# Attention output computed transposed: values stationary, probabilities moving, two heads on the array's column halves

## The chip, the cores and the metric

The kernel runs on one core of a Trainium2 chip. The metric is the device time of one execution in microseconds (us), the median of several runs. The engines are TensorE (PE: matmuls, with their weight loads listed as PEld), VectorE (DVE), ScalarE (ACT), GpSimd (POOL) and the DMA queue of SyncE (SP).

## The reference

For each of 32 batch elements: x is 256 rows of 256, the context 77 rows of 256. Both are layer-normalized; queries come from x, keys and values from x and context together (333 keys). There are 4 heads of 64. Queries and keys are RMS-normalized per head, context keys may be masked, and softmax attention follows:

```python
sim = einsum('bhid,bhjd->bhij', qn, kn)
attn = softmax(where(mask, sim, -max), axis=-1)
out = einsum('bhij,bhjd->bhid', attn, v)
x = x + out.reshape(b, n, 256) @ W_out + b_out
x = x + ffn(layernorm(x))
```

The feed-forward part is a mixture of 8 experts (squared ReLU, 128 inner columns each, the best two of a group by a sigmoid router) and a shared expert of 512 inner columns.

## The kernel before, in words

The kernel makes 32 steps, one for each batch element (B = 32). A step b does the attention of element b, the feed-forward part of element b-1, and the projections (keys, values, queries) of element b+1. The order of instructions on each engine is written out by hand in the five `step` functions; engines meet only through semaphores, whose counts are computed from b. Steps 0, 1 and 31 are written out, steps 2 to 30 are the body of one loop (`steps`, line 212).

Sizes: P = 128; S = 256 query rows make T = 2 tiles; D = 256 makes FT = 2 feature tiles of two heads each; 333 keys make CH = 3 chunks of KC = 111. A unit u is one tile of 128 queries for one head; there are U = 8 of them, u = 4 t + h. A pair is two units of the same tile, with heads 2 ft and 2 ft + 1.

Most matrix products are split (`split_product`, line 258): both operands are held as a high and a low part of type fp32r, and three matmuls (L261, L262, L263) add up. The transposes, and the product of probabilities and values, work on plain fp32.

Attention of a step, in the order of TensorE: transposes of the normalized keys (L321), sums of query squares (L309), four score pairs (L342, L344, L346; the two heads of a pair use the upper and the lower 64 rows of the array), then per unit u the transposes of its probabilities (`transpose_probs`, L356), three chunks of 128 x 111, and `probs_times_v` (L367), which has the transposed probabilities stationary and the 64 value columns of the head moving, so that unit u fills 64 columns of the bank `attn_ps[:, 3]`. After unit 7 DVE multiplies the whole bank by the inverse row sums (`attn_out`, L834), TensorE transposes the result (`transpose_attn`, L380), ACT takes the high parts (L626), DVE the low parts (`attn_low`, L840), and `project_out` (L384) multiplies with W_out into the bank `attn_ps[:, 3]`. DVE adds the residual (L848) and makes the second layer norm.

Between these pieces stand, in TensorE's queue, those of the feed-forward part: `up(p)` for six pairs of hidden tiles (12 matmuls of 256 columns), the shared expert's `down_shared` (12 matmuls each), `down_expert(e)` (6 matmuls each), and, towards the end of the step, the next element's `transpose_ln` (L275, L276), `project_kv` of the key chunks 1, 2 and 0 (6 matmuls of 512 columns each) and `project_q`.

ACT copies the transposed probabilities out of PSUM (`pt_out`, L618, ring `probs_t`, 3 slots), makes the exponentials (`softmax`, L611, with the row sums as a by-product), the ReLU and its square (`hidden`, L644, L649), and the next element's scaled normalized rows (`ln_full`, L570). DVE's queue has, after the scores are masked (`mask_scores`, L815) and among router steps: `layer_norm1`, additions of the experts' results (`add_expert`, L972), the rounding of hidden values (`hidden_high`, L957), `ln_high` (L760), then `invert_sums` (L827, the reciprocal of 8 row sums per partition), `add(4)`, `attn_out`, `add(5)`, `attn_low`, `k_norms` (L780, L785), `layer_norm2`. POOL makes low parts of hidden values and inverse roots.

Of the kernel before, what the change touches and what calls it, by code (L numbers as in the profile page):

```python
# [22 lines left out]
ALU = mybir.AluOpType  # L23
# [10 lines left out]
def build(nc, x, ctx_in, mask, g_x, b_x, g_l, b_l, q_gamma, k_gamma, w_q, w_kv, w_out, b_out,  # L34
          gate_t, gate_bias, up_t, down_t, out):
    B, S, D = x.shape
# [20 lines left out]
    with ExitStack() as stack:  # L57
# [59 lines left out]
        row_inv = sb("row_inv", [P, U])  # L117
        PT_RING = 3
        SCORE_RING = 4
        probs_t = sb("probs_t", [KC, PT_RING, CH * P])  # L120
        attn = sb("attn", [P, U, DH])
# [60 lines left out]
        score_ps, pt_ps, pv_ps = sem("score_ps"), sem("pt_ps"), sem("pv_ps")  # L182
        at_ps, out_ps, x2t_ps, logit_ps = sem("at_ps"), sem("out_ps"), sem("x2t_ps"), sem("logit_ps")
# [5 lines left out]
        prob_done, pt_done = sem("prob_done"), sem("pt_done")  # L189
# [15 lines left out]
        PARTS = (slice(1, 3), slice(0, 1))  # L205
        LN1_STEPS = 2 * (T + 1)
# [15 lines left out]
        def _(sp):  # L222
# [28 lines left out]
            steps(sp, step)  # L251
# [5 lines left out]
        def _(pe):  # L257
# [102 lines left out]
            def probs_times_v(b, u, first):  # L360
                if u == 0:
# [10 lines left out]
            def transpose_attn(b, following):  # L372
                pe.wait_ge(attn_done, b + 1)
# [4 lines left out]
                for ft in range(FT):  # L378
                    for t in range(T):
                        last = nc.tensor.transpose(up_ps[:, ft, t * P:(t + 1) * P],  # L380
                                                   attn[:, t * H + 2 * ft:t * H + 2 * ft + 2, :], ident[:])
                    last.then_inc(at_ps, 1)

            def project_out(b):  # L384
                pe.wait_ge(at_hi_done, (b + 1) * FT)
                pe.wait_ge(at_lo_done, (b + 1) * FT)
                for t in range(T):
                    for k in range(FT):
                        cols = slice(t * P, (t + 1) * P)
                        last = split_product(attn_ps[:, 3, t * D:(t + 1) * D], (at_hi[:, k, cols], at_lo[:, k, cols]),  # L390
                                             (w_hi[:, k, 3 * D:4 * D], w_lo[:, k, 3 * D:4 * D]), k == 0, k == FT - 1)
                last.then_inc(out_ps, 1)
# [72 lines left out]
            def step(b, experts, following):  # L465
# [773 lines left out]
```

## Time and profile before

| | us |
|---|---|
| median of 3 runs | 1362.79 |
| lowest and highest | 1362.51, 1364.13 |
| the profiled execution, its own time | 1370.73 |
| its span, first to last instruction | 1368.9 |
| PE busy, weight loads busy | 1286.9, 1194.2 |
| DVE, ACT, POOL busy | 1022.7, 747.5, 539.4 |
| L367, products of probabilities and values (1536 passes) | 205.7 |
| L356, transposes of probabilities (768) | 132.5 |

How to read it: busy time is what an engine's instructions cover. Matmuls are pipelined, and their ends are modelled, so that the starts of successive ones say more than their durations. A row of the timeline gives the start, the duration from the first start to the last end, engine, line, operation, what is written and read, shapes, and how many instructions were merged; in brackets stands how long the engine was idle before it and what ended that.

### The profile page before, as it was taken

The numbers are of one execution on the slowest core, as the hardware profiler recorded it, in microseconds if no ns is written. First come the engines' busy times: TensorE is split into PE (matmuls) and PEld (weight loads), VectorE is DVE, ScalarE is ACT, GpSimd is POOL, SyncE is SP. The second block draws the span as 40 slices with busy tenths as digits, with TensorE's granted clock in tenths as the row PEclk, the third lists the DMA queues.
The fourth block names the chain that finished last, engine by engine and source line by source line (L and its number), as shares of the span: only waits on it lengthen the run. The fifth ranks groups of instructions, "written<-read, shape, count | busy, mean of one in ns | idle before, by whom it ended". The sixth has DMA issues, their size and how long they took to land.

```text
span 1368.9 us, 33442 instructions
## 1 busy us (share of the span) xinstructions
PE 1286.9 (94%) x10176; PEld 1194.2 (87%) x10176; DVE 1022.7 (75%) x3465; ACT 747.5 (55%) x1701; POOL 539.4 (39%) x477
## 2 busy tenths in 40 slices
PE   3799999999999999999999999999999999999997
PEld 2788899898899898899898899888889889889986
DVE  3478777788777778777778877777877778877765
ACT  3465555565555565555565555555555556555552
POOL 4143443343443343344343343333444334444332
PEclk9599999999999999999999999999999999999998
DMA  4000000000000000000000000000000000000000
GB/s 137 11 12 20 19 18 0 18 18 18 18 18 0 18 18 18 18 18 8 10 18 18 18 18 8 10 18 18 18 18 13 5 18 18 18 18 18 0 9 16
DMA packets 28099, 24.20 MB, mean 18 GB/s; under 512 B 6640, under 2 KB 27536, under 8 KB 28080
## 3 DMA queue, kind: packets, MB, share of 16 engines
q1 hardware_dynamic: 27744, 23.83, 5.5%
q0 software_dynamic: 336, 0.14, 0.2%
q8 instruction: 10, 0.16, 0.0%
q14 instruction: 9, 0.07, 0.0%
HBM read 15.57 MB, written 8.39 MB: 18 GB/s over the span
## 4 chain that ended last, share of the span: by engine, by line
PE 68%; DVE 13%; issue 12%; ACT 4%; DVEq 1%; POOL 1%; DMA 1%; POOLq 0%; ACTq 0%
PE attn_ps L367 13%; PE up_ps L261 6%; PE up_ps L263 6%; PE up_ps L262 6%; PE down_ps L261 5%; PE attn_ps L356 5%; PE attn_ps L261 5%; PE attn_ps L262 4%; PE attn_ps L263 4%; PE down_ps L263 4%; PE down_ps L262 4%; DVE masked L815 4%; PE attn_ps L309 2%; ACT relu L649 2%; ACT relu_sb L644 1%
## 5 line engine op out<-in xcount | busy, mean ns | idle before, releaser
L1148 POOL TENSOR_TENSOR hid_lo<-relu,hid_hi 128x512 fp32r<-128x512 f32 x192 | 246.6, 1284 | 485.1 <-DVE hid_hi L957 485.1
L261 PE MATMUL down_ps<-down_hi,hid_hi 128*128 128x256 f32 x768 | 238.4, 310 | 17.7 <-POOL hid_lo L1148 16.1
L972 DVE SCALAR_TENSOR_TENSOR acc<-down_ps,route_w,acc 128x256 f32<-128x256 f32 x512 | 222.0, 476 | 22.4 <-PE down_ps L263 17.7
L261 PE MATMUL up_ps<-x_hi,up_hi 128*128 128x256 f32 x768 | 230.3, 300 | 1.2 <-ACT x_hi L633 1.0
L263 PE MATMUL down_ps<-down_hi,hid_lo 128*128 128x256 f32 x768 | 215.9, 281 | 0.0
L262 PE MATMUL down_ps<-down_lo,hid_hi 128*128 128x256 f32 x768 | 215.7, 281 | 0.0
L262 PE MATMUL up_ps<-x_lo,up_hi 128*128 128x256 f32 x768 | 215.5, 281 | 0.0
L263 PE MATMUL up_ps<-x_hi,up_lo 128*128 128x256 f32 x768 | 215.5, 281 | 0.0
L367 PE MATMUL attn_ps<-v_sb,probs_t 111*128 111x64 f32 x1536 | 205.7, 275 | 10.0 <-DVE row_max L815 9.3
L611 ACT ACTIVATE probs<-masked,neg_max,q_scale 128x333 f32<-128x333 f32 x256 | 167.8, 656 | 79.0 <-DVE neg_max L822 79.0
L367 PEld LDWEIGHTS attn_ps<-v_sb,probs_t 111*128 111x128 f32 x1536 | 194.7, 196 | 16.8 <-DVE row_max L815 15.6
L957 DVE CAST hid_hi<-relu 128x512 fp32r<-128x512 f32 x192 | 113.9, 593 | 113.8 <-ACT relu L649 113.7
L644 ACT ACTIVATE relu_sb<-up_ps 128x512 f32<-128x512 f32 x192 | 114.7, 597 | 142.9 <-PE up_ps L263 141.0
L261 PEld LDWEIGHTS down_ps<-down_hi,hid_hi 128*128 128x128 f32 x768 | 145.6, 190 | 32.9 <-issue 32.9
L1105 POOL TENSOR_TENSOR k_scale<-k_norm,minus_half 111x8 f32<-111x8 f32 x64 | 84.5, 1322 | 186.0 <-DVE k_norm L785 186.0
L618 ACT ACTIVATE probs_t<-attn_ps 111x384 f32<-111x384 f32 x256 | 124.4, 486 | 59.1 <-PE attn_ps L356 59.1
L261 PEld LDWEIGHTS up_ps<-x_hi,up_hi 128*128 128x128 f32 x768 | 146.4, 191 | 8.0 <-issue 6.6
L356 PE MATMUL attn_ps<-ident,probs 128*111 128x128 f32 x768 | 132.5, 283 | 15.6 <-DVE row_max L815 14.7
L262 PEld LDWEIGHTS up_ps<-x_lo,up_hi 128*128 128x128 f32 x768 | 146.4, 191 | 0.0
L263 PEld LDWEIGHTS up_ps<-x_hi,up_lo 128*128 128x128 f32 x768 | 146.2, 190 | 0.0
L262 PEld LDWEIGHTS down_ps<-down_lo,hid_hi 128*128 128x128 f32 x768 | 145.8, 190 | 0.0
L263 PEld LDWEIGHTS down_ps<-down_hi,hid_lo 128*128 128x128 f32 x768 | 144.6, 188 | 0.0
(145 smaller groups left out, 2819.3 us busy)
## 6 DMA issues: line engine op xcount, KB each, us to landing
x_in<-in_x SPq DMA_DIRECT2D x32, 256.0 KB, 2.7
out<-acc SPq DMA_DIRECT2D x32, 256.0 KB, 2.2
c_in<-in_ctx SPq DMA_DIRECT2D x32, 77.0 KB
up_stage<-in_up_t SPq DMA_DIRECT2D x1, 1536.0 KB, 12.1
down_stage<-in_down_t SPq DMA_DIRECT2D x1, 1536.0 KB, 15.0
mask_in<-in_mask SPq DMA_DIRECT2D x32, 9.6 KB, 2.8
w_stage<-in_w_kv SPq DMA_DIRECT2D x1, 512.0 KB, 5.8
w_stage<-in_w_q SPq DMA_DIRECT2D x1, 256.0 KB, 5.1
```

The lines of the kernel that those rows point to most:

```text
L261: nc.tensor.matmul(out_ap, s_hi, m_hi, start=first, stop=False)
L262: nc.tensor.matmul(out_ap, s_hi, m_lo, start=False, stop=False)
L263: return nc.tensor.matmul(out_ap, s_lo, m_hi, start=False, stop=last)
L356: last = nc.tensor.transpose(attn_ps[0:KC, u % PT_RING, c * P:(c + 1) * P], probs[:, u, c * KC:(c + 1) * KC], ident[:])
L367: last = nc.tensor.matmul(attn_ps[:, 3, u * DH:(u + 1) * DH], probs_t[:, u % PT_RING, c * P:(c + 1) * P], v_sb[:, c, h * DH:(h + 1) * DH], ...
L611: nc.scalar.activation(probs[:, u, :], masked[:, u, :], ACT.Exp, bias=neg_max[:, u:u + 1], scale=q_scale[:, u:u + 1], accum_out=row_sum[:, ...
L618: nc.scalar.activation(probs_t[:, u % PT_RING, :], attn_ps[0:KC, u % PT_RING, 0:CH * P], ACT.Copy).then_inc(pt_done, 1)
L644: nc.scalar.activation(relu_sb[:, p % 2, :], up_ps[:, p % 2, :], ACT.Relu).then_inc(relu_done, 1)
L957: nc.vector.tensor_copy(hid_hi[:, p % HID_RING, :], relu2[:, p % 2, :]).then_inc(hid_hi_done, 1)
L972: nc.vector.scalar_tensor_tensor(acc[:, t, :], down_ps[:, (e + 1) % 2, t * D:(t + 1) * D], route_w[:, t, e:e + 1], acc[:, t, :], ALU.mult, ...
L1105: nc.gpsimd.tensor_tensor(dst, src, minus_half[0:src.shape[0], 0:src.shape[1]], ALU.pow).then_inc(done, 1)
L1148: nc.gpsimd.tensor_tensor(hid_lo[:, p % HID_RING, :], relu2[:, p % 2, :], hid_hi[:, p % HID_RING, :], ALU.subtract).then_inc(hid_lo_done, 1)
```

## The change

1. `probs_times_v` works on pairs. The values of a head (111 x 64) are stationary, the transposed probabilities (111 x 128) move. The two heads of a pair write to the partitions 0 to 63 and 64 to 127 of the same bank and the same columns, so each uses one half of the array's columns. The result is already transposed: features on partitions, queries along the free dimension.
2. The inverse row sums must then vary along the free dimension. `invert_sums` is called once per query tile and writes each inverse 64 times (128 x 4 x 64). `spread_inverse` (4 transposes on TensorE, in `up_ps[:, 0]`) turns them, `inverse_out` (ACT) copies them to `inv_t`, and `attn_out` multiplies by that. `transpose_attn` is gone.
3. `attn_high` and `attn_low` work by query tile, out of SBUF. `project_out` is called once per tile, and writes to `up_ps[:, 1]`; the second call stands after the projection of chunk 2.
4. The ring of transposed probabilities in SBUF has 4 slots instead of 3 (`PT_SB`); that in PSUM keeps 3.
5. The loop is gone: all 32 steps are written out.

```diff
-        row_inv = sb("row_inv", [P, U])
+        row_inv = sb("row_inv", [P, U, DH])
...
-        def steps(eng, step):
-            step(0, False, True)
-            step(1, True, True)
-            with eng.Fori(2, B - 1) as b:
-                step(b, True, True)
-            step(B - 1, True, False)
+        def steps(step):
+            for b in range(B):
+                step(b, b > 0, b < B - 1)
...
-            def probs_times_v(b, u, first):
...
-                pe.wait_ge(pt_done, b * U + u + 1)
-                h = u % H
+            def probs_times_v(b, pair):
+                t, ft = divmod(pair, FT)
...
+                pe.wait_ge(pt_done, b * U + 2 * pair + 2)
+                cols = slice(ft * S + t * P, ft * S + (t + 1) * P)
                 for c in range(CH):
-                    last = nc.tensor.matmul(attn_ps[:, 3, u * DH:(u + 1) * DH],
-                                            probs_t[:, u % PT_RING, c * P:(c + 1) * P],
-                                            v_sb[:, c, h * DH:(h + 1) * DH], start=(c == 0), stop=(c == CH - 1))
+                    for i in range(2):
+                        h = 2 * ft + i
+                        last = nc.tensor.matmul(attn_ps[i * DH:(i + 1) * DH, 3, cols],
+                                                v_sb[:, c, h * DH:(h + 1) * DH],
+                                                probs_t[:, (2 * pair + i) % PT_SB, c * P:(c + 1) * P],
+                                                start=(c == 0), stop=(c == CH - 1))
...
+            def spread_inverse(b, following):
+                pe.wait_ge(row_inv_done, (b + 1) * T)
+                if following:
+                    pe.wait_ge(ln_full_done, (b + 1) * FT + 1)
+                else:
+                    pe.wait_ge(relu_done, b * PAIRS)
+                for t in range(T):
+                    for ft in range(FT):
+                        u = t * H + 2 * ft
+                        last = nc.tensor.transpose(up_ps[:, 0, ft * S + t * P:ft * S + (t + 1) * P],
+                                                   row_inv[:, u:u + 2, :], ident[:])
+                last.then_inc(inv_ps, 1)
...
                 transpose_probs(b, 1)
-                probs_times_v(b, 0, first)
                 ffn("down", 0)
                 transpose_probs(b, 2)
-                probs_times_v(b, 1, first)
+                probs_times_v(b, 0)
                 ffn("up", 4)
                 transpose_probs(b, 3)
-                probs_times_v(b, 2, first)
                 ffn("down", 1)
                 transpose_probs(b, 4)
-                probs_times_v(b, 3, first)
+                probs_times_v(b, 1)
                 ffn("down", 2)
                 transpose_probs(b, 5)
                 ffn("up", 5)
-                probs_times_v(b, 4, first)
                 ffn("down", 3)
+                probs_times_v(b, 2)
                 if following:
                     transpose_ln(b + 1, experts)
-                probs_times_v(b, 5, first)
                 transpose_probs(b, 6)
                 ffn("down", 4)
                 transpose_probs(b, 7)
                 ffn("down", 5)
-                probs_times_v(b, 6, first)
-                probs_times_v(b, 7, first)
+                spread_inverse(b, following)
+                probs_times_v(b, 3)
                 if following:
                     project_kv(b + 1, 1)
-                transpose_attn(b, following)
+                project_out(b, 0, following)
                 if following:
                     project_kv(b + 1, 2)
-                project_out(b)
+                project_out(b, 1, following)
                 if following:
                     project_kv(b + 1, 0)
...
+            def inverse_out(b, first):
+                act.wait_ge(inv_ps, b + 1)
...
+                nc.scalar.activation(inv_t[:], up_ps[:, 0, :].rearrange("p (f s) -> p f s", f=FT),
+                                     ACT.Copy).then_inc(inv_done, 1)
...
-            def invert_sums(b):
-                dve.wait_ge(prob_done, b * U + U)
-                nc.vector.reciprocal(row_inv[:], row_sum[:]).then_inc(row_inv_done, 1)
+            def invert_sums(b, t, first):
+                cols = slice(t * H, (t + 1) * H)
+                dve.wait_ge(prob_done, b * U + (t + 1) * H)
+                if not first:
+                    dve.wait_ge(inv_ps, b)
+                nc.vector.reciprocal(row_inv[:, cols, :], row_sum[:, cols].unsqueeze(2)
+                                     .to_broadcast([P, H, DH])).then_inc(row_inv_done, 1)
...
                 routing(18)
+                invert_sums(b, 0, first)
                 add(0)
...
                     ln_high(b + 1, False)
-                invert_sums(b)
+                invert_sums(b, 1, first)
                 add(4)
                 attn_out(b, first)
                 add(5)
-                attn_low(b)
+                attn_low(b, 0)
+                attn_low(b, 1)
```

## Rows read from the trace of the kernel before

**Rows 1.** Busy time by stretch, one whole step of the loop (x: instructions).
```profile
core 0: us, PE busy (x) PEld busy (x) DVE busy (x) ACT busy (x) POOL busy (x), PEclk, DMA share, GB/s
...
604.30:645.15 40.85, 39.53 (x320) 36.75 (x319) 31.66 (x109) 23.07 (x53) 16.64 (x14) 1.00 0.05 15
```

**Rows 2.** Timeline of PE: key transposes and first probability transposes, loop and last step.
```profile
604.34 0.74 PE L321 MATMUL attn_ps<-ident,k_rms 111*128 111x111 f32 x6
...
618.11 0.58 PE L356 MATMUL attn_ps<-ident,probs 128*111 128x128 f32 x3 [0.54 <-DVE row_max L815]
...
1298.72 0.74 PE L321 MATMUL attn_ps<-ident,k_rms 111*128 111x111 f32 x6
...
1312.29 0.55 PE L356 MATMUL attn_ps<-ident,probs 128*111 128x128 f32 x3 [0.59 <-ACT probs L611]
```

**Rows 3.** Timeline of PE, 624.5 to 639.1 of the same step, in part.
```profile
624.58 0.49 PE L356 MATMUL attn_ps<-ident,probs 128*111 128x128 f32 x3
624.90 0.78 PE L367 MATMUL attn_ps<-v_sb,probs_t 111*128 111x64 f32 x6
625.49 0.36 PE L261 MATMUL down_ps<-down_hi,hid_hi 128*128 128x256 f32 x1
625.69 0.28 PE L262 MATMUL down_ps<-down_lo,hid_hi 128*128 128x256 f32 x1
...
631.10 0.38 PE L275 MATMUL up_ps<-ident,x_hat 128*128 128x128 f32 x2
...
634.47 1.45 PE L367 MATMUL attn_ps<-v_sb,probs_t 111*128 111x64 f32 x12
635.73 0.46 PE L261 MATMUL attn_ps<-w_hi,ln_hi 128*111 128x512 f32 x1
...
637.20 0.60 PE L380 MATMUL up_ps<-ident,attn 128*128 128x128 f32 x4
...
639.04 0.31 PE L261 MATMUL attn_ps<-w_hi,at_hi 128*128 128x256 f32 x1
```

**Rows 4.** Timeline of PE around one score pair.
```profile
614.26 0.28 PE L262 MATMUL down_ps<-down_lo,hid_hi 128*128 128x256 f32 x1
614.38 0.28 PE L263 MATMUL down_ps<-down_hi,hid_lo 128*128 128x256 f32 x1
614.59 0.42 PE L342 MATMUL attn_ps<-k_hi,q_hi 64*128 64x334 f32 x2
614.85 0.31 PE L344 MATMUL attn_ps<-k_lo,q_hi 64*128 64x334 f32 x2
615.00 0.31 PE L346 MATMUL attn_ps<-k_hi,q_lo 64*128 64x334 f32 x2
615.24 0.38 PE L261 MATMUL down_ps<-down_hi,hid_hi 128*128 128x256 f32 x1
```

**Rows 5.** Timeline of ACT: copies of transposed probabilities, units 1 and 3.
```profile
621.30 0.47 ACT L618 ACTIVATE probs_t<-attn_ps 111x384 f32<-111x384 f32 x1
...
625.94 0.47 ACT L618 ACTIVATE probs_t<-attn_ps 111x384 f32<-111x384 f32 x1
```

**Rows 6.** Groups of DVE by form, ten steps: busy us, mean ns.
```profile
L901 DVE RECIPROCAL score<-sig_den 128x16 f32<-128x16 f32 x10 | 2.5, 253 | 0.3
...
L827 DVE RECIPROCAL row_inv<-row_sum 128x8 f32<-128x8 f32 x10 | 1.9, 195 | 0.0
...
L945 DVE RECIPROCAL pick_inv<-pick_eps 128x2 f32<-128x2 f32 x10 | 1.5, 151 | 0.0
```

**Rows 7.** Timeline of DVE, 631 to 638, in part.
```profile
631.21 0.43 DVE L957 CAST hid_hi<-relu 128x512 fp32r<-128x512 f32 x1 [2.05 <-ACT relu L649]
...
633.50 0.19 DVE L827 RECIPROCAL row_inv<-row_sum 128x8 f32<-128x8 f32 x1
...
636.01 0.69 DVE L834 TENSOR_TENSOR attn<-attn_ps,row_inv 128x512 f32<-128x512 f32 x1 [1.43 <-issue]
636.62 0.87 DVE L972 SCALAR_TENSOR_TENSOR acc<-down_ps,route_w,acc 128x256 f32<-128x256 f32 x2
```

**Rows 8.** Timeline of DVE: the residual addition.
```profile
640.69 0.69 DVE L848 TENSOR_TENSOR x<-attn_ps,x_res 128x512 f32<-128x512 f32 x1
```

More of the change, by code:

```diff
@@ L205, in build @@
         PARTS = (slice(1, 3), slice(0, 1))
+        PV = U // 2
         LN1_STEPS = 2 * (T + 1)
@@ L249, in step @@
                     store(b - 1)
-            steps(sp, step)
+            steps(step)
             store(B - 1)
@@ L377, in transpose_attn @@
                     pe.wait_ge(relu_done, b * PAIRS)
[L378 to L392, printed above, removed]
+                pe.wait_ge(at_hi_done, b * T + t + 1)
+                pe.wait_ge(at_lo_done, b * T + t + 1)
+                for k in range(FT):
+                    cols = slice(t * P, (t + 1) * P)
+                    last = split_product(up_ps[:, 1, t * D:(t + 1) * D], (at_hi[:, k, cols], at_lo[:, k, cols]),
+                                         (w_hi[:, k, 3 * D:4 * D], w_lo[:, k, 3 * D:4 * D]), k == 0, k == FT - 1)
+                if t == T - 1:
+                    last.then_inc(out_ps, 1)
             def transpose_x2(b):
@@ L538, in _ @@
             project_q(0)
-            steps(pe, step)
+            steps(step)
             up(B - 1, 0, False, False)
@@ L615, in pt_out, with attn_high @@
                 act.wait_ge(pt_ps, b * U + u + 1)
-                if not first or u >= PT_RING:
-                    act.wait_ge(pv_ps, b * U + u + 1 - PT_RING)
-                nc.scalar.activation(probs_t[:, u % PT_RING, :], attn_ps[0:KC, u % PT_RING, 0:CH * P],
+                if not first or u >= PT_SB:
+                    act.wait_ge(pv_ps, b * PV + (u - PT_SB) // 2 + 1)
+                nc.scalar.activation(probs_t[:, u % PT_SB, :], attn_ps[0:KC, u % PT_RING, 0:CH * P],
                                      ACT.Copy).then_inc(pt_done, 1)
-            def attn_high(b, first):
+            def inverse_out(b, first):
+                act.wait_ge(inv_ps, b + 1)
+                if not first:
+                    act.wait_ge(attn_done, b)
+                nc.scalar.activation(inv_t[:], up_ps[:, 0, :].rearrange("p (f s) -> p f s", f=FT),
+                                     ACT.Copy).then_inc(inv_done, 1)
+            def attn_high(b, t, first):
+                act.wait_ge(attn_done, b + 1)
                 if not first:
                     act.wait_ge(out_ps, b)
-                for ft in range(FT):
-                    act.wait_ge(at_ps, b * FT + ft + 1)
-                    nc.scalar.activation(at_hi[:, ft, :], up_ps[:, ft, 0:S], ACT.Copy).then_inc(at_hi_done, 1)
+                cols = slice(t * P, (t + 1) * P)
+                nc.scalar.activation(at_hi[:, :, cols], attn[:, :, cols], ACT.Copy).then_inc(at_hi_done, 1)
             def x2_high(b, first):
@@ L686, in step @@
                 pt_out(b, 7, first)
-                attn_high(b, first)
+                inverse_out(b, first)
+                attn_high(b, 0, first)
+                attn_high(b, 1, first)
                 if following:
@@ L703, in _ @@
             q_out(0, True)
-            steps(act, step)
+            steps(step)
             hidden(B - 1, 0, False)
@@ L823, in negate_max, with attn_low @@
                                                ALU.mult, ALU.mult).then_inc(neg_max_done, 1)
[L825 to L827 removed]
+            def invert_sums(b, t, first):
+                cols = slice(t * H, (t + 1) * H)
+                dve.wait_ge(prob_done, b * U + (t + 1) * H)
+                if not first:
+                    dve.wait_ge(inv_ps, b)
+                nc.vector.reciprocal(row_inv[:, cols, :], row_sum[:, cols].unsqueeze(2)
+                                     .to_broadcast([P, H, DH])).then_inc(row_inv_done, 1)
             def attn_out(b, first):
[L830 to L831 removed]
+                dve.wait_ge(inv_done, b + 1)
+                dve.wait_ge(pv_ps, (b + 1) * PV)
                 if not first:
[L833 to L841 removed]
+                    dve.wait_ge(at_hi_done, b * T)
+                nc.vector.tensor_tensor(attn[:], attn_ps[:, 3, :].rearrange("p (f s) -> p f s", f=FT), inv_t[:],
+                                        ALU.mult).then_inc(attn_done, 1)
+            def attn_low(b, t):
+                dve.wait_ge(at_hi_done, b * T + t + 1)
+                cols = slice(t * P, (t + 1) * P)
+                nc.vector.tensor_tensor(at_lo[:, :, cols], attn[:, :, cols], at_hi[:, :, cols],
+                                        ALU.subtract).then_inc(at_lo_done, 1)
             def layer_norm2(b, first):
@@ L1082, in _ @@
             dve.wait_ge(gamma_done, 1)
-            steps(dve, step)
+            steps(step)
             f = B - 1
@@ L1198, in _ @@
             k_scales(0, 1, True)
-            steps(pool, step)
+            steps(step)
             for p in range(PAIRS):
```

33 lines of the change are left out of this document (12 added, 21 removed).

## The prediction

> **What bounds the kernel now.** I read the busy time of one step first [rows 1]: of the 40.85 us of a step of the loop TensorE (PE) is busy 39.5, VectorE (DVE) 31.7, ScalarE (ACT) 23.1 and GpSimd (POOL) 16.6, at granted clock 1.00. Then the step's period: the key transposes stand at 604.34 and, 17 steps later, at 1298.72 [rows 2], so 40.85 us each. TensorE bounds the kernel, its instruction order is the schedule, and any wait that opens in it is paid in full. So the working is a walk along TensorE's order through one step, in two stretches: from the first transpose of probabilities (T0, 618.11) to the transposes of the next step's normalized rows (Tln, 631.10), 12.99 us [rows 2, 3]; and from Tln to the end of the output projection, which starts at 639.04 and has 12 products at 0.12, so to 640.44, 9.34 us after Tln [rows 3]. The cadence 0.12 is 614.26 to 614.38 [rows 4].
>
> **What a product of probabilities and values costs now.** One unit starts at 624.90 and the next product at 625.49: six passes (each fp32 matmul is two load and multiply passes) in 0.59 us. The matmul after it is followed by the next only after 0.20 instead of 0.12, so leaving costs 0.08 [rows 3]. Two units are 1.18, with what is left of the exits 1.2 to 1.35 per pair.
>
> **What a pair will cost.** Twelve passes, each with half the stationary columns and twice the moving ones. If the two column halves run side by side, they take the time of six. How long an fp32 pass of 128 moving columns takes is not shown: at least 0.06 (256 columns follow each other at 0.12), at most 0.2 (a pass of 64 takes 0.10, doubled). The nearest row is the fp32 transpose, which also moves 128 columns: three between 624.58 and 624.90, 0.11 each [rows 3]. I take 0.11, body 0.66. The array must also go in and out of a divided mode. The score products do that by row halves [rows 4]: 0.21 before the first pair instead of 0.12, 0.26 to the second instead of 0.15, and 0.24 after the last instead of 0.15, so 0.29, and 0.08 for the exit. A pair is 0.66 + 0.37 = 1.03 us; lower bound 0.36 + 0.08 = 0.44 (cheapest pass, no cost of the mode), upper bound 12 x 0.11 + 0.37 = 1.69 (halves one after the other; a pass of 0.2 side by side comes to about the same). The gain on four pairs is therefore about 1 us a step. The Trainium skill says (TensorEngine Tiling, Key Properties) that a change of tiling mode drains TensorE, a rule that speaks against four new islands; by rows 4 the trace agrees. The same page (Theoretical Speedup) promises up to 2x for swapping operands with column tiling; a pair would then be 0.59 + 0.08 = 0.67, and the sum below 19 us instead of 60.
>
> **First stretch.** T0, up(3), T1, down(0), T2 need 0.33 + 1.48 + 0.33 + 0.78 + 0.33: PE is at 621.38. Pair 0 needs the transposed probabilities of units 0 and 1, and ACT copies unit 1 at 621.30 for 0.47 [rows 5], behind its ReLU and square; pair 0 starts at 621.83, after a stall of 0.45 (the old first unit waited for DVE there; that wait goes). End 622.86, up(4) to 624.26. Pair 1 needs unit 3, which lands 1.83 after the end of up(4) (625.94 + 0.47 against 624.58) [rows 3, 5], so 626.15 with the semaphore; PE is done with T3, down(1), T4 at 625.70: another 0.45. Pair 1 to 627.18, down(2), T5, up(5), down(3) 3.21, pair 2 from 630.39 to 631.42. Tln stands 0.3 later than before: the two stalls eat the gain. The four-slot ring of transposed copies doesn't bind (its slots are freed by pair 0 before unit 4 is copied, at about 626.5).
>
> **Second stretch, from Tln = 0.** The reciprocal of the row sums takes 0.151, 0.195 and 0.253 us for 2, 8 and 16 elements [rows 6]: 7.3 ns an element, on three points in a line. The change lets it write 4 x 64 elements per call (each inverse repeated 64 times), twice a step: 0.151 + 254 x 0.0073 = 2.0 us each, 4.0 a step in place of 0.2. The bounds are 0.4 (if it went like other DVE work) and 2.0. The first call is covered. It comes at about 623.4, and DVE still idles 2.05 us before it rounds the last pair's hidden values [rows 7]; what it delays on the way (two additions, the next step's rows, pair 4's high part) TensorE asks for 2 us or more later. If that cover were gone, it would cost up to 2.0 a step. The second call has no cover: it stands behind the rounding of the next step's rows, and starts 2.40 after Tln (633.50) [rows 7]; it ends at 4.4. TensorE's new transposes of the inverses wait for it. PE reaches them after Tln, T6, down(4), T7, down(5) = 634.47 - 631.10 less the unit of 0.6 that stood in between = 2.8 [rows 3], and stalls 1.65, with pair 3 and the next keys' projection queued behind. Transposes 4 x 0.11 to 4.85; pair 3 to 5.88; key projection 1.47 (635.73 to 637.20) to 7.35. ACT's copy of the inverses (384 wide 0.47 [rows 5], so 512 wide 0.63) is done at 5.7, under pair 3; ACT has room for it [rows 1]. DVE's multiply starts 0.28 after a pair's body (636.01 against 635.73) [rows 3, 7], at 6.08, 0.61 long; the next expert's addition follows it in the queue, 0.87 [rows 7], then the low part of the first half, about 0.4: 7.95. The first half of the output projection starts at 8.0, a stall of 0.65 where there was none, since the chain has only one key projection as cover where it had two and four transposes. Then 0.70 + 1.5 + 0.70: 10.9 instead of 9.34, so +1.55. Removing the result's transposes gains nothing, as four transposes of inverses take their place. 
>
> **After it.** Between the second key projection and the end of the output projection stands now one half (0.70), not two. DVE's key sums wait for the former and stand ahead of the residual addition in its queue; that addition already starts at 640.69, 0.25 after the projection [rows 8]. It will come up to 0.7 later after the projection, and with it the second normalization, the queries' low part and the next up(0). Bounds 0 and 0.7; I take the middle, 0.35, as some slack is there.
>
> **The steps written out.** The last step is already written out: T0 comes 13.57 after its key transposes, in the loop 13.77 [rows 2]. I take 0.2 less per step. Bounds: 0 (the last step has no successor to load) and 0.2; fetching more instructions costs nothing visible in the written-out last step. The DMAs issued stay the same.
>
> **Sum.** +0.3 + 1.55 + 0.35 - 0.2 = +2.0 us a step, in 30 steps +60. The first and the last step pay the reciprocals where TensorE waits anyway and save transposes on a bare chain: I put them at 0. The profiled execution took 1370.7 (span 1368.9 and 1.8 around it), so 1430.7; the median of the runs is 7.9 below it, hence 1423. With pair P the sum is 2.0 - 3.75 x (1.03 - P) a step.
>
> **Rivals.**
> - *The halves are nearly free.* P = 0.44: the first stretch falls by 1.5 in all, the second rises by 1.1, after it 0, loop -0.2: -0.6 a step, 1345. It decides at P = 0.50; below that the kernel is faster in spite of the reciprocal. For it: the score pairs show two row halves of 334 columns in 0.15, so halves can overlap. Against: the same rows show the price of the mode, which alone leaves 0.13 for twelve passes. Chance 0.10.
> - *The halves don't overlap,* or a pass takes 0.2: P = 1.6 to 1.7, +4.1 to +4.5 a step, 1485 to 1497. For it: the passes are issued two of one half and then two of the other, not alternating like the score pairs. Against: a half that is free while the other works should still take its next pass. Chance 0.10.
> - *The reciprocal is cheap for wide outputs* (0.4 us): the stall at the transposes of the inverses falls away, that in front of the projection stays; +0.4 a step, 1375. Against: three points in a line. Chance 0.08.
> - *No net change* (the change doesn't do what it says): P near 0.5, or old waits for DVE that vanish as new ones open; 1360 to 1366. Chance 0.05.
>
> **How the numbers follow.** The forecast itself, P from 0.75 to 1.3, has 0.67 and gives 1391 to 1453. The range takes in the cheap reciprocal and no net change below, and goes up to P = 1.4: 1360 to 1465; the two rivals beyond it have 0.2 together. About 0.2% is what a measurement of this kernel can tell from no change. Faster 0.10, same 0.05, slower 0.85.
>
> **What would show each step.** Right: RECIPROCAL 128x256 at 2.0 us, 64 times; TensorE idle about 1.6 us a step before the transposes of row_inv, released by DVE's reciprocal, and about 0.6 before the output projection, released by at_lo; waits for probs_t before pairs 0 and 1; a pair from its first pass to the next product in about 1 us; period near 42.9. Wrong: a pair under 0.6 us, a reciprocal under 1 us, or a period below 41.2. The prediction falls if the inverses are ready before TensorE asks for them, or if the clock drops in the new gaps.

## The result, and the profile after

The kernel with the change takes 1457.14 us (median of 4 runs, 1453.61 to 1458.92); the kernel before, run beside it, 1363.46. The ratio is 1.064 (95% interval 1.0606 to 1.0675). The profiled executions stand 85.9 us apart (1456.6 and 1370.7; the spans 1454.5 and 1368.9). The executions of the kernel before fall into two groups, near 1363 us at a mean clock of 0.990 and near 1370.5 at 0.984, the profiled one in the second, so sizes are compared below by steps rather than by ratios. The forecast was 1423 in a range of 1360 to 1465: the sign and the waits that it named came out, and the loss is about half as large again as forecast, above the 1391 to 1453 to which the prediction gave a chance of 0.67.

From the page of the kernel after: the busy time of each engine, the clock, and one group.

```profile
PE 1282.6 (88%) x10176; PEld 1129.3 (78%) x10176; DVE 1112.6 (76%) x3497; ACT 763.3 (52%) x1733; POOL 536.4 (37%) x477
...
L369 PE MATMUL attn_ps<-probs_t,v_sb 111*64 111x128 f32 x1536 | 117.5, 289 | 27.0 <-ACT probs_t L624 27.0
```

The products of probabilities and values are busy 117.5 us instead of 205.7, and yet the kernel is slower: PE was busy for 94% of its span before (1286.9 of 1368.9) and is now for 88%. So the loss is in waits (and PE's busy time is itself drawn out by the stretches of lower clock shown below). Which ones, the waits of PE say (us in total, times, longest):

```profile
PE up_ps L385 <- DVE row_inv L845: 62.2, 32, 3.3
PE attn_ps L369 <- ACT probs_t L624: 27.0, 64, 0.6
```

The first is the one forecast: the transposes of the inverse row sums (L385) wait for the reciprocal. One step in PE's timeline, from the first transpose of probabilities (T0) to the end of the output projection, answers to [rows 2, 3]:

```profile
565.92 0.55 PE L355 MATMUL attn_ps<-ident,probs 128*111 128x128 f32 x3 [0.59 <-ACT probs L617]
...
569.72 0.88 PE L369 MATMUL attn_ps<-probs_t,v_sb 111*64 111x128 f32 x12 [0.46 <-ACT probs_t L624]
570.53 0.38 PE L260 MATMUL up_ps<-x_hi,up_hi 128*128 128x256 f32 x1
570.75 0.28 PE L261 MATMUL up_ps<-x_lo,up_hi 128*128 128x256 f32 x1
...
573.95 0.88 PE L369 MATMUL attn_ps<-probs_t,v_sb 111*64 111x128 f32 x12 [0.37 <-ACT probs_t L624]
...
577.89 0.28 PE L262 MATMUL down_ps<-down_hi,hid_lo 128*128 128x256 f32 x1
578.10 0.88 PE L369 MATMUL attn_ps<-probs_t,v_sb 111*64 111x128 f32 x12
578.90 0.44 PE L274 MATMUL up_ps<-ident,x_hat 128*128 128x128 f32 x2
...
583.73 0.66 PE L385 MATMUL up_ps<-ident,row_inv 128*128 128x128 f32 x4 [1.93 <-DVE row_inv L845]
584.32 0.88 PE L369 MATMUL attn_ps<-probs_t,v_sb 111*64 111x128 f32 x12
585.12 0.49 PE L260 MATMUL attn_ps<-w_hi,ln_hi 128*111 128x512 f32 x1
...
587.25 0.36 PE L260 MATMUL up_ps<-w_hi,at_hi 128*128 128x256 f32 x1 [0.47 <-DVE at_lo L859]
...
589.46 0.28 PE L260 MATMUL up_ps<-w_hi,at_hi 128*128 128x256 f32 x1
```

A pair: 0.21 from the last product before it (577.89) instead of 0.12, 0.80 from its first pass to the next instruction, and 0.22 to the one after (570.53 to 570.75), 0.10 over the cadence. So 0.09 + 0.80 + 0.10 = 0.99 us. On DVE the same stretch reads, as an answer to [rows 6, 7]:

```profile
578.80 0.43 DVE L976 CAST hid_hi<-relu 128x512 fp32r<-128x512 f32 x1 [2.17 <-ACT relu L662]
...
580.50 0.34 DVE L775 CAST ln_hi<-ln_t 128x333 fp32r<-128x333 f32 x1 [0.48 <-ACT ln_t L576]
581.20 0.82 DVE L775 CAST ln_hi<-ln_t 128x333 fp32r<-128x333 f32 x1 [0.36 <-ACT ln_t L576]
581.94 1.74 DVE L845 RECIPROCAL row_inv<-row_sum 128x256 f32<-128x256 f32 x1
583.60 0.77 DVE L991 SCALAR_TENSOR_TENSOR acc<-down_ps,route_w,acc 128x256 f32<-128x256 f32 x2
585.30 0.69 DVE L853 TENSOR_TENSOR attn<-attn_ps,inv_t 128x512 f32<-128x512 f32 x1 [0.93 <-ACT inv_t L631]
```

Behind the reciprocal, 1.74 us long, DVE goes on at 583.60 and PE at 583.73. The table by stretches then shows what has no term in the forecast's sum (two neighbouring steps, and four pieces of the second; after the busy times stands PE's granted clock):

```profile
core 0: us, PE busy (x) PEld busy (x) DVE busy (x) ACT busy (x) POOL busy (x), PEclk, DMA share, GB/s
552.02:595.27 43.25, 38.89 (x320) 34.21 (x319) 34.49 (x110) 23.59 (x55) 16.53 (x14) 1.00 0.05 16
595.27:639.32 44.05, 40.15 (x319) 35.32 (x319) 34.42 (x110) 23.59 (x55) 16.54 (x14) 0.96 0.05 15
624.00:627.00 3.00, 1.06 (x10) 0.86 (x9) 2.64 (x4) 1.15 (x4) 1.80 (x2) 1.00 0.02 5
627.00:628.00 1.00, 1.00 (x10) 0.83 (x12) 0.59 (x2) 0.35 (x1) 0.00 (x0) 0.91 0.00 0
628.00:631.00 3.00, 3.00 (x15) 2.12 (x12) 2.03 (x5) 0.97 (x3) 0.00 (x0) 0.50 0.00 0
631.00:632.00 1.00, 1.00 (x8) 0.88 (x7) 0.11 (x1) 0.00 (x0) 0.00 (x0) 0.88 0.00 0
```

In the second step PE had stood for 1.94 us before the transposes of the inverses, as it does in every step, and then the granted clock fell to 0.50, its level of 1.2 GHz, for about 3.4 us. The key projection shows it in its starts:

```profile
626.96 0.66 PE L385 MATMUL up_ps<-ident,row_inv 128*128 128x128 f32 x4 [1.94 <-DVE row_inv L845]
627.54 1.33 PE L369 MATMUL attn_ps<-probs_t,v_sb 111*64 111x128 f32 x12
628.80 0.77 PE L260 MATMUL attn_ps<-w_hi,ln_hi 128*111 128x512 f32 x1
629.36 0.63 PE L261 MATMUL attn_ps<-w_lo,ln_hi 128*111 128x512 f32 x1
629.79 0.63 PE L262 MATMUL attn_ps<-w_hi,ln_lo 128*111 128x512 f32 x1
...
631.38 0.28 PE L260 MATMUL up_ps<-w_hi,at_hi 128*128 128x256 f32 x1
```

They follow each other at 0.43 us, at full clock at 0.23. The last row shows that the wait of 0.47 before the output projection is absent in such a step: the slower key projection has covered it, so not all of the slow stretch is lost. Of the 30 steps, 10 keep the full clock and take 43.22 us (one of them 43.58), and 20 have a stretch at the lower clock and take 44.05. In 19 of these it comes behind the wait for the inverses; in the first it stands in the key transposes. Before, a step took 40.85 at full clock [rows 1, 2].

### The profile page after: what moved, and what is told of

Same layout as the page of the kernel before. It is cut to its first block and busy times, and to the rows that moved or that the text cites. A ratio compares the mean times of both kernels' runs of the same rounds, so it can differ in the third digit from the quotient of the medians.

```text
span 1454.5 us, 29534 instructions
## 1 busy us (share of the span) xinstructions
PE 1282.6 (88%) x10176; PEld 1129.3 (78%) x10176; DVE 1112.6 (76%) x3497; ACT 763.3 (52%) x1733; POOL 536.4 (37%) x477
## 3 DMA queue, kind: packets, MB, share of 16 engines
q8 instruction: 83, 1.36, 0.4%
## 5 line engine op out<-in xcount | busy, mean ns | idle before, releaser
L260 PE MATMUL down_ps<-down_hi,hid_hi 128*128 128x256 f32 x768 | 235.2, 306 | 14.9 <-issue 12.6
L991 DVE SCALAR_TENSOR_TENSOR acc<-down_ps,route_w,acc 128x256 f32<-128x256 f32 x512 | 216.0, 465 | 7.9 <-PE down_ps L262 7.8
L976 DVE CAST hid_hi<-relu 128x512 fp32r<-128x512 f32 x192 | 122.0, 635 | 105.9 <-ACT relu L662 105.9
L369 PE MATMUL attn_ps<-probs_t,v_sb 111*64 111x128 f32 x1536 | 117.5, 289 | 27.0 <-ACT probs_t L624 27.0
L624 ACT ACTIVATE probs_t<-attn_ps 111x384 f32<-111x384 f32 x256 | 120.6, 487 | 38.5 <-PE attn_ps L355 38.5
L662 ACT ACTIVATE relu<-relu_sb 128x512 f32<-128x512 f32 x192 | 121.4, 632 | 6.1
```

Of the source, the lines that this page charges most:

```text
L260: nc.tensor.matmul(out_ap, s_hi, m_hi, start=first, stop=False)
L369: last = nc.tensor.matmul(attn_ps[i * DH:(i + 1) * DH, 3, cols], v_sb[:, c, h * DH:(h + 1) * DH], probs_t[:, (2 * pair + i) % PT_SB, c * P ...
L624: nc.scalar.activation(probs_t[:, u % PT_SB, :], attn_ps[0:KC, u % PT_RING, 0:CH * P], ACT.Copy).then_inc(pt_done, 1)
L662: nc.scalar.activation(relu2[:, p % 2, :], relu_sb[:, p % 2, :], ACT.Square).then_inc(relu2_done, 1)
L976: nc.vector.tensor_copy(hid_hi[:, p % HID_RING, :], relu2[:, p % 2, :]).then_inc(hid_hi_done, 1)
L991: nc.vector.scalar_tensor_tensor(acc[:, t, :], down_ps[:, (e + 1) % 2, t * D:(t + 1) * D], route_w[:, t, e:e + 1], acc[:, t, :], ALU.mult, ...
```

## The experiments

The theory: the loss is the wait for the second reciprocal, with the key projection and the output projection queued behind it, and the clock fall that this wait brings. The rivals: the new pairs themselves cost the time, or the writing out of the steps does, or the length of the reciprocal rather than its place.

**The second reciprocal earlier.** Only the place of one call in DVE's queue differs from the kernel after.

```diff
+                invert_sums(b, 1, first)
                 high(5)
                 add(3)
                 if following:
                     ln_high(b + 1, False)
-                invert_sums(b, 1, first)
```

> The changed kernel with one line moved in DVE's queue: the second wide reciprocal stands before the rounding of the last pair's hidden values, where DVE idled 2.17 us, instead of behind the rounding of the next step's rows. Theory (the late reciprocal is what TensorE waits for, and the idle it leaves lets the clock fall): the wait before the transposes of the inverses goes from 1.9 us to under 0.1, no step has a stretch at clock 0.5, the period is 41.3 to 41.5 us and the time 1380 to 1390 us; a wait of about 0.5 before the output projection stays. Rival 1 (the clock falls because the passes on column halves leave half of the array idle): the wait goes, but two steps in three keep their stretch at 0.5, about 1400 us. Rival 2 (something else, ACT's copy or POOL, is late right behind the reciprocal): a wait of over 1 us stays before the transposes or before pair 3, over 1410 us.

Measured: 1369.91 us (10 runs; 1.0032 of before, 1.0011 to 1.0054), a step 41.07, and from step 2 to step 30 no stretch at the lower clock, though the pairs use the column halves as before. That is 10 us less than was expected: a step is 2.15 shorter than a full-clock step of the kernel after, more than the wait of 1.93. DVE takes the call into the idle time in front of `high(5)` (625.77), and PE finds the inverses ready:

```profile
625.77 1.74 DVE L845 RECIPROCAL row_inv<-row_sum 128x256 f32<-128x256 f32 x1
```
```profile
630.87 0.60 PE L385 MATMUL up_ps<-ident,row_inv 128*128 128x128 f32 x4
```

The instruction costs the same 1.74 us and is as frequent. So of the change's 94 us, 87 hang on the place of one instruction in a queue.

**The reciprocal narrow, the repetition by a copy.**

```diff
-                nc.vector.reciprocal(row_inv[:, cols, :], row_sum[:, cols].unsqueeze(2)
-                                     .to_broadcast([P, H, DH])).then_inc(row_inv_done, 1)
+                nc.vector.reciprocal(inv_small[:, cols], row_sum[:, cols]).then_inc(small_done, 1)
+                dve.wait_ge(small_done, b * T + t + 1)
+                nc.vector.tensor_copy(row_inv[:, cols, :], inv_small[:, cols].unsqueeze(2)
+                                      .to_broadcast([P, H, DH])).then_inc(row_inv_done, 1)
```

> The changed kernel in its own order, but each wide reciprocal (256 elements, 1.74 us) is a reciprocal of 4 elements and a copy that repeats each 64 times. By the cost per element of the reciprocal: 0.17 and about 0.4 us, so the inverses come 1.1 us earlier in a step; the wait falls from 1.9 to about 0.8 us, period about 42.1, and 1400 to 1410 us if the shorter idle leaves the clock up, 1420 to 1425 if it still falls in two steps of three. Rival (the broadcast read is what is slow, not the division): the copy takes over 1 us as well, and the time stays above 1435 us.

Measured: 1418.07 us (1.0393, 1.0351 to 1.0435), a step 42.54: between the 1400 to 1410 of the expectation and the 1435 of its rival. The copy takes 0.99 us in the second call and 1.31 in the first, but that is not its own price:

```profile
47.77 0.30 DVE L849 COPY row_inv<-inv_small 128x256 f32<-128x256 f32 x1
...
599.58 1.31 DVE L849 COPY row_inv<-inv_small 128x256 f32<-128x256 f32 x1
...
610.42 0.99 DVE L849 COPY row_inv<-inv_small 128x256 f32<-128x256 f32 x1
```
```profile
599.45 1.28 POOL L1173 TENSOR_TENSOR hid_lo<-relu,hid_hi 128x512 fp32r<-128x512 f32 x1 [6.14 <-DVE hid_hi L980]
...
610.38 0.89 POOL L1141 TENSOR_TENSOR ln_lo<-ln_t,ln_hi 128x333 fp32r<-128x333 f32 x1 [0.27 <-DVE ln_hi L777]
```
```profile
611.47 0.66 PE L387 MATMUL up_ps<-ident,row_inv 128*128 128x128 f32 x4 [1.38 <-DVE row_inv L849]
```

In 63 of the 64 calls one of POOL's subtractions has started before the copy, and the copy ends 0.15 us after it (610.38 + 0.89 and 610.42 + 0.99; 599.45 + 1.28 and 599.58 + 1.31). In the one call in which none runs, at 47.77, the same copy takes 0.30. So it is not the repeating read that is slow here: the copy is held until POOL's instruction is through. The wide reciprocal shows no such thing; it takes 1.74 whether POOL works beside it for 1.7 us or for 0.4.

The wait of PE shrinks only from 1.94 to 1.38, and with 1.38 the clock stays up in all steps. So the step is 0.68 shorter than a full-clock step of the kernel after (0.55 is the wait), 20 us in 30 steps, and the other half of the gain of 39 is the clock: 20 steps longer by 0.83 us are 17 us.

**The wait filled with work.** Fourteen products of 256 columns are put into the wait, in steps 1 to 30; their result is not used.

```diff
             def spread_inverse(b, following):
+                if following:
+                    pe.wait_ge(ln_full_done, (b + 2) * FT)
+                    if b > 0:
+                        for k in range(14):
+                            nc.tensor.matmul(up_ps[:, 1, 0:S], w_hi[:, 0, 0:P], w_hi[:, 1, 0:S], start=True, stop=True)
                 pe.wait_ge(row_inv_done, (b + 1) * T)
```

> The changed kernel with 14 needless products of 256 columns (about 1.65 us) that TensorE does in its wait before the transposes of the inverses; everything else is as it was. Theory (the clock falls because TensorE idles 1.9 us there): all steps take 43.2 us, granted clock 1.00 throughout, about 1440 us, faster by about 17 us through more work. Rival (the clock falls because of the column halves): the stretches at 0.5 stay, 1455 us or more.

Measured: 1439.4 us (1.0543, 1.0501 to 1.0585), every step 43.2, clock 0.989 over the span where the kernel after has 0.963; PE still waits 0.25 for the inverses behind the filler. PE does more, the inverses come when they did, and the kernel is 17.7 us faster. This is the fall of the clock alone, and it is the price worked out from the steps.

**The kernel before with its steps written out.** `steps` as in the change, nothing else.

> The kernel before with all 32 steps written out, nothing else. The prediction said 0.2 us less per step: 1357 us, period 40.65. The rival, by the changed kernel's trace (the first probability transposes stand 13.9 us after the key transposes there, against 13.8 in the loop of before): no difference, 1363 us, period 40.85.

Measured: 1356.23 us (10 runs; 0.9938, 0.9911 to 0.9964), a step 40.56, so 0.29 less; T0 stands 13.57 behind its key transposes in nearly all of them, as in the last step before [rows 2].

**The kernel of the first experiment with the loop restored.**

> The kernel with the moved reciprocal, with the loop of the kernel before (steps 2 to 30). Writing the steps out gave 0.29 us a step without the rest of the change (40.85 to 40.56). If it is worth the same here: period 41.36. Rival: the new waits hide it, 41.1.

Measured: 1373.34 us in one run, a step 41.23 instead of 41.07, halfway between the expected 41.36 and the rival. The loop costs 0.16 here: part of it is hidden, as the wait before the output projection falls from 0.40 to 0.23.

**The two heads of a pair one after the other.** In the kernel of the first experiment; the same twelve passes, in another order.

```diff
-                for c in range(CH):
-                    for i in range(2):
+                for i in range(2):
+                    for c in range(CH):
                         h = 2 * ft + i
```

> The kernel with the moved reciprocal; in a pair the six passes of one head come first, then the six of the other, instead of two and two; column halves as they were. A pair took 0.80 us from its first pass to the next product. If the halves work at the same time only when their passes alternate: 12 x 0.11 + 0.2 = about 1.4 us, period up by 2 us or more (43). If what limits a pair is loading 64 columns at a time, one load after the other in any order: 0.8 again, period 41.1.

**Both heads on the same half of the columns.** In that order, and from step 1 on both heads write to the partitions 0 to 63. Half of the attention result is then left out: the second head overwrites the first, and the partitions 64 to 127 of the bank hold what other pieces of the step wrote there.

```diff
-                        last = nc.tensor.matmul(attn_ps[i * DH:(i + 1) * DH, 3, cols],
+                        last = nc.tensor.matmul(attn_ps[(i * DH if b == 0 else 0):(i * DH + DH if b == 0 else DH), 3, cols],
```

> As m7_head_after_head, but from the second step on both heads of a pair use the lower column half (the output leaves out half of the attention result, and mixes in old values). If the halves work at the same time, this takes it away: over 1.3 us a pair, period over 43. If the loads in a row are the limit, the same time as m7_head_after_head within 0.1 us a pair.

Measured: 1406.14 and 1452.83 us, one run each, a step 42.12 and 43.64. The body of an undisturbed pair is 0.80 in alternating order, 1.08 head after head (595.51 to 596.59) and 1.45 on one half (576.75 to 578.20):

```profile
595.51 1.14 PE L369 MATMUL attn_ps<-probs_t,v_sb 111*64 111x128 f32 x12 [0.38 <-ACT probs_t L624]
596.59 0.39 PE L260 MATMUL down_ps<-down_hi,hid_hi 128*128 128x256 f32 x1
```
```profile
576.75 1.52 PE L369 MATMUL attn_ps<-probs_t,v_sb 111*64 111x128 f32 x12
578.20 0.44 PE L274 MATMUL up_ps<-ident,x_hat 128*128 128x128 f32 x2
```

On one half a pass of 128 moving columns takes 1.45 / 12 = 0.12; the prediction had 0.11. With two halves in turn twelve passes take 0.80, 0.65 less. So the halves do overlap: the four pairs save 4 x 0.65 = 2.6 a step against one half, which is the difference of the steps (43.64 - 41.07 = 2.57). Alternation is not all of it. Head after head came out between the two times expected for it, 1.4 and 0.8: the same order on two halves is 0.37 faster than on one, and alternating brings the other 0.28. Where the 0.37 arise is not shown.

**The halves of the projection together.** In the kernel of the first experiment; both come after the key projection of chunk 2.

```diff
                 if following:
-                project_out(b, 0, following)
-                if following:
                     project_kv(b + 1, 2)
+                project_out(b, 0, following)
                 project_out(b, 1, following)
```

> The kernel with the moved reciprocal (41.07 us a step), with both halves of the output projection behind the second key projection, as in the kernel before. Theory (splitting them took their cover away and put the key sums in front of the residual addition): the wait for the low parts, 0.4 us a step, goes, and the key transposes and the first probability transposes come 0.35 and 0.3 us earlier in the step; period 40.0 to 40.3, 1336 to 1346 us, faster than the kernel before even with its steps written out (1356). Rival (the 0.3 and 0.35 come from somewhere else, such as the later copy of the inverses or DVE's longer queue): only the wait goes, period 40.65, about 1357 us.

Measured: 1330.29 us (0.9732, 0.9695 to 0.977), a step 39.75: 1.32 less than with the first edit alone. The wait before the projection (0.40) is gone, from the end of the projection to the next key transposes it is 4.63 instead of 5.10, and T0 stands 13.65 behind its key transposes instead of 13.89. This is faster than both kernels. Against the kernel before with its steps written out (a step 40.56) the gain is 0.81 a step; the other 0.29 of the 1.10 come from writing the steps out. What is left of PE's waits in some 15 steps is the pair's (12.7 us over 30 pairs):

```profile
PE attn_ps L369 <- ACT probs_t L624: 12.7, 30, 0.5
```

**The halves together, the reciprocal where the change has it.** The same edit in the kernel after.

> The changed kernel with both halves of the output projection behind the second key projection, the reciprocal where the change put it. If the two causes add up: 1.3 us a step less than 43.22 in the steps at full clock, since the moved reciprocal's kernel lost that much too; the wait of 1.9 us for the inverses stays and with it the fall of the clock in some steps; 1410 to 1420 us. Rival (the stall for the inverses hides part of it, as DVE catches up meanwhile): under 0.9 us a step less, over 1428 us.

Measured: 1416.53 us (1.0349, 1.031 to 1.0387). Steps of 41.8 at full clock and of 43.3 with a fall mostly alternate; 14 of the 30 have one. In full-clock steps the edit saves 1.4, about the 1.3 that it saved above, so the two edits add up. The wait for the inverses stays at 1.94, and with it the falls, each now dearer (1.5 us for 0.83): here no step has a wait before the output projection that the slow stretch could cover, which is 0.47 of the difference.

**Pairs 0 and 1 later.** In the faster kernel, pair 0 comes after `up(4)` and pair 1 after `down(2)`.

> The kernel with the moved reciprocal and the projection's halves together (39.75 us a step), with pairs 0 and 1 one feed-forward piece later in TensorE's queue: pair 0 behind up(4), pair 1 behind down(2). Theory (TensorE waits 0.47 and 0.38 us a step there for ACT's copies of units 1 and 3, which stand behind a ReLU and its square): both waits go, period 38.9, about 1304 us. Rival (ACT is at its limit in this stretch, so the waits only move to pair 2 or to the copies' PSUM ring): period above 39.4, over 1318 us.

Measured: 1326.33 us (0.969, 0.9655 to 0.9725), a step 39.61 instead of 39.75, though both waits for `probs_t` (0.85 a step) are gone. A new one has come:

```profile
561.93 0.35 PE L260 MATMUL down_ps<-down_hi,hid_hi 128*128 128x256 f32 x1 [0.63 <-DVE acc L991]
```
```profile
559.35 1.74 DVE L845 RECIPROCAL row_inv<-row_sum 128x256 f32<-128x256 f32 x1
561.02 0.77 DVE L991 SCALAR_TENSOR_TENSOR acc<-down_ps,route_w,acc 128x256 f32<-128x256 f32 x2
```

`down(2)` writes where `add(0)` still has to read, and `add(0)` stands behind the first reciprocal. The first call was covered only as long as PE came late.

**The first reciprocal behind two additions.** In the kernel of the last experiment.

```diff
-                invert_sums(b, 0, first)
                 add(0)
                 if following:
                     normalize1(b + 1, False)
                 add(1)
+                invert_sums(b, 0, first)
                 high(4)
```

> The last kernel (39.61 us a step), with the first wide reciprocal behind the additions of experts 0 and 1 instead of ahead of them. In that kernel the waits for ACT's copies went, but TensorE waits 0.6 us a step before down(2) for the addition of expert 0, which stands behind the 1.74 us reciprocal: the prediction called that call covered, and it is only while TensorE comes late. Theory: the wait goes and nothing takes its place; period 39.0, about 1307 us. Rival (DVE is the bound of this stretch, in whatever order): a wait for the hidden values' parts or another addition takes its place, period above 39.4.

Measured: 1333.32 us (0.9747, 0.9707 to 0.9786), 7 us slower, a step 39.90. The wait before `down(2)` is gone, and one before `down(5)` stands in its place:

```profile
573.67 0.36 PE L260 MATMUL down_ps<-down_hi,hid_hi 128*128 128x256 f32 x1 [0.56 <-DVE acc L991]
```
```profile
568.02 1.74 DVE L845 RECIPROCAL row_inv<-row_sum 128x256 f32<-128x256 f32 x1
569.67 0.36 DVE L976 CAST hid_hi<-relu 128x512 fp32r<-128x512 f32 x1
569.95 0.86 DVE L991 SCALAR_TENSOR_TENSOR acc<-down_ps,route_w,acc 128x256 f32<-128x256 f32 x2
570.73 1.74 DVE L845 RECIPROCAL row_inv<-row_sum 128x256 f32<-128x256 f32 x1
```

Between the two calls is now 1.06 us (569.67 to 570.73) for one cast and `add(2)`; `add(3)` and the next step's rows come after both, and PE waits 0.56 before `down(5)` and 0.37 before the key projection. What this order gains at one place it gives back at the next. From T0 to the high parts of the next step's rows, DVE's longest idle times in the kernel with pairs 0 and 1 later are 0.62 and 0.49 us, against two calls of 1.74; that DVE is the limit of this stretch is argued from this, not shown.

## Why the prediction came out too low

The walk can be laid beside the trace, in us from T0 (first four) and from the transposes of the normalized rows (the rest):

| | forecast | measured |
|---|---|---|
| pair 0 starts | 3.72 | 3.80 |
| pair 1 starts | 8.04 | 8.03 |
| pair 2 starts | 12.28 | 12.18 |
| transposes of the normalized rows | 13.3 | 12.98 |
| second reciprocal starts | 2.40 | 3.04 |
| transposes of the inverses | 4.4 | 4.83 |
| pair 3 starts | 4.85 | 5.42 |
| output projection starts | 8.0 | 8.35 |
| it ends | 10.9 | 11.27 |

**The pair** came out in sum, 0.99 for 1.03, but by luck: the body takes 0.80 where 0.66 was forecast, and going in and out costs 0.19 where 0.37 was taken over from the score pairs. On one half it is 1.45 + 0.19 = 1.64, near the upper bound of 1.69. The rivals "nearly free" and "don't overlap" fell with it. By the up to 2x of the Trainium skill (TensorEngine Tiling, Theoretical Speedup) the prediction's estimate was 0.67, with a sum below 19 us (by its own formula 19.5); the trace does not reach it, as the body alone takes 0.80. With the drain of the same page's Key Properties the trace agrees: 0.09 in and 0.10 out.

**The first stretch** went as walked: the two waits for `probs_t` (0.46 and 0.37, forecast 0.45 each) eat what three pairs save. It came out at no change where +0.3 was forecast: the last pair starts 0.10 earlier than in the walk, and the transposes behind it start 0.80 after it, where the walk put the whole 1.03, mode included.

**The reciprocal** was put at 2.0 us and takes 1.74. From 2 elements to 256 that is (1.74 - 0.15) / 254 = 6.3 ns an element; the line through 2, 8 and 16 [rows 6] gave 7.3. The 2.3 us that the prediction estimated by the Trainium skill (VectorE: DVE Perf Modes, First, the fixed hardware budget) are further off. But the call starts 0.64 later than forecast, and this outweighs it. The prediction took the start from the old order, 2.40 behind the transposes [rows 7]. The rows' high parts now come later (580.50 and 581.20, so 1.60 and 2.30 behind, before 1.39 and 2.15), and the second takes 0.82 for 0.34 while POOL's low part of the first runs beside it:

```profile
580.92 0.91 POOL L1137 TENSOR_TENSOR ln_lo<-ln_t,ln_hi 128x333 fp32r<-128x333 f32 x1 [0.33 <-DVE ln_hi L775]
```

That POOL holds the cast is read from the times, no run removes POOL's part. The times are clear, though: all 32 times the cast ends 0.19 after that instruction of POOL (580.92 + 0.91 and 581.20 + 0.82), as the copies of the second experiment end 0.15 after theirs. The wait is 1.93 for 1.65, the one before the projection 0.47 for 0.65, and the stretch ends +1.93 later than before, forecast +1.55.

**After it** the forecast was +0.35. Measured from the end of the projection to the next key transposes are 5.10 instead of 4.75, and from there to T0 13.89 instead of the 13.57 of written-out steps: +0.67, near the upper bound of 0.7. The cause named in the prediction, the second half of the projection too close to the residual addition, is borne out by the run with the halves together: the 5.10 are back at 4.63, and T0 at 13.65.

**The loop**: -0.29 for -0.2, by the run of the kernel before with its steps written out.

**The sum** of a full-clock step is then 0 + 1.93 + 0.67 - 0.29 = 2.31 against the forecast 2.0, and the trace has 43.22 - 40.85 = 2.37. That is 71 us for 30 steps, where 60 were forecast. **The step that failed** is what the sum has no term for: the clock. The prediction named a drop of the clock in the new gaps as a thing at which it would fall, and by that sign it has fallen. It gave the drop no price, though its own wait of 1.65 us was longer than all the time in which PE is idle in a step of before (40.85 - 39.53 = 1.32) [rows 1]. It costs 20 x 0.83 = 17 us (17.7 by the fillers). 71 + 17 = 88. The profiled executions stand 86 apart, since that of the kernel before loses about 4 us more at its start (the second key transposes stand at 73.87, in the kernel after at 69.72). Its clock is at the lower level there for 34.1 us, in the kernel after for 20.5 (second view, with the columns of the table by stretches):

```profile
33.53:67.66 34.13, 26.32 (x117) 23.63 (x118) 17.51 (x44) 14.41 (x32) 4.45 (x5) 0.50 0.04 11
```
```profile
30.49:50.97 20.48, 11.58 (x68) 9.46 (x67) 16.64 (x40) 11.54 (x25) 3.74 (x3) 0.50 0.07 18
```

The medians stand 94 apart, as this execution of the kernel before was 7 us above its median.

**The first call** was said to be covered. It is, in the kernel after; the two last experiments show on what that rests.

Which steps have the fall is open: the wait before is 1.93 or 1.94 in either kind. With fillers, and with a wait of 1.38, it is gone; no run looked for the point between.

## What to carry to other kernels

Where a change makes one instruction wide, look first for an idle stretch in its queue: a reciprocal of 1.74 us a step cost 87 us of kernel in one place, and no wait at all three pieces earlier. A new wait of PE near 2 us is to be priced twice, once for the wait and once for the matmuls behind it at the lower clock, and a filler is a quick test for the second. Where a DVE instruction looks dear, see what POOL does beside it before blaming its form. Two halves of the array overlapped here, most when their passes alternate, but entering and leaving the divided mode (0.19 a pair) and the waits that open in front of a faster piece can take the gain: here it came only after two moves in the order, at 0.973 of the time before.

## What the runs showed of the hardware that was not expected

- The granted clock fell to 1.2 GHz behind an idle time of 1.94 us in 19 of 30 steps (14 of 30 in the kernel with only the halves together), for about 3.4 us, and never behind 1.38 us.
- The same fall costs 0.83 us a step where a wait of 0.47 stands behind it that the slow matmuls cover, and 1.5 where there is none; the wait is 0.47 of that difference, the rest is open.
- A DVE copy of 128 x 256 that repeats each of 4 values 64 times took 0.30 us with no subtraction of POOL beside it, and 0.99 or 1.31 where one had started before it: it then ended 0.15 us after POOL's. The wide reciprocal took 1.74 with 1.7 us of POOL's work beside it and with 0.4.
- Twelve fp32 passes of 128 columns: 0.80 us in turn on two column halves, 1.08 head after head, 1.45 on one half.
- The loop costs 0.16 to 0.29 us a step against the written-out kernels. Written out, the instruction queues bring 1.36 and 0.52 MB instead of 0.16 and 0.07, with no wait that every step has. But single steps in the written-out kernels are about 0.35 us longer than their neighbours (43.58 for 43.22), which no step from 3 to 30 of the two looped kernels is; the cause was not looked for.
